# Layer 0: own scores and softmax of the next sequence ahead of the output products, output products in the projections' PSUM banks

## The reference, cut to what matters

```
xn   = layernorm(x)
q, k, v = xn Wq, xn Wk, xn Wv            # 8 heads of 64
own  = softmax(q k^T / 8) within segments of 32 rows, times v
mem  = elu1(q) . (sum over earlier segments of elu1(k)^T v) / (elu1(q) . z)     # elu1 = elu + 1
att  = sigmoid(beta) * mem + (1 - sigmoid(beta)) * own
h    = layernorm(gelu(xn Wfc)) * w + b;  s = h Wproj       # ternary Wfc, Wproj
x    = x + (s * sigmoid(s)) * (att Wo)
```

## Time and profile before

| | |
|---|---|
| median of 3 runs | 3017.87 us (3016.2 to 3020.25) |
| the profiled execution's own time | 3017.2 us |
| its span | 3015.1 us, of which layer 0's loop is about 79 to 575 us |
| TensorE, VectorE, ScalarE, GpSimd busy over the span | 83%, 77%, 57%, 11% |
| mean granted TensorE clock | 0.857 of full |

### The profile page before, as it was taken

How to read it: one execution, slowest core, us unless ns; L and a number is a source line. 1 busy time by engine, 2 the same in 40 slices (tenths; PEclk the granted TensorE clock), 3 DMA queues, 4 the chain that set the end, 5 groups by cost and what they waited for, 6 DMA issues and landing times. The chain is left out here.

```text
span 3015.1 us, 55454 instructions
## 1 busy us (share of the span) xinstructions
PE 2503.6 (83%) x18812; PEld 1895.3 (63%) x18812; DVE 2326.8 (77%) x6048; ACT 1709.8 (57%) x3452; POOL 329.3 (11%) x356
## 2 busy tenths in 40 slices
PE   1888888799999999967728888888888888988886
PEld 1555565577777777756725666666666666666665
DVE  2777777788788888767237888888888888888887
ACT  1676766565566565644325565565565655656554
POOL 0000000000000000023140111111111111111111
PEclk9999999899999999988857777777777778777778
DMA  7000000000000000030112334343333343432334
GB/s 215 1 0 0 0 0 0 0 1 1 1 0 0 1 0 1 1 82 14 56 43 76 94 85 106 92 107 98 80 78 87 96 106 92 106 91 78 86 86 112
DMA packets 86517, 163.71 MB, mean 54 GB/s; under 512 B 18856, under 2 KB 45616, under 8 KB 86320
## 3 DMA queue, kind: packets, MB, share of 16 engines
q0 software_dynamic: 20480, 62.93, 11.0%
q1 hardware_dynamic: 64640, 98.15, 10.0%
q10 hardware_dynamic: 1200, 0.27, 0.1%
HBM read 92.60 MB, written 9.99 MB: 34 GB/s over the span
## 5 line engine op out<-in xcount | busy, mean ns | idle before, releaser
L1132 ACT ACTIVATE b_neg<-b_neg,b_nmax 128x128 f32<-128x128 f32 (+1 forms) x512 | 190.9, 444 | 210.7 <-DVE b_nmax L1286 210.7
L2535 ACT ACTIVATE d_probs<-l_bank,w_b 128x256 f32<-128x256 f32 x512 | 210.2, 468 | 156.2 <-PE l_bank L2373 153.6
L2798 DVE TENSOR_TENSOR_SCAN d_state<-w,d_state 128x1024 f32<-128x1024 f32 x128 | 290.9, 2283 | 5.0 <-issue 3.7
L2373 PE MATMUL l_bank<-xnT,w_w 128*128 128x256 f32 x1024 | 245.1, 382 | 14.4 <-ACT d_probs L2535 14.4
L2384 PE MATMUL l_bank<-w_w,d_probs 128*128 128x128 f32 x2048 | 252.7, 276 | 0.0
L2384 PEld LDWEIGHTS l_bank<-w_w,d_probs 128*128 128x128 f32 x2048 | 244.9, 192 | 11.7 <-ACT d_probs L2535 5.3
L2303 PE MATMUL l_bank<-w 9*128 9x256 f32 x1040 | 207.5, 669 | 25.0 <-ACT w L2458 18.9
L2497 ACT ACTIVATE w<-d_delta,d_negA 128x255 f32<-128x255 f32 x520 | 220.2, 499 | 0.0
L94 POOL TENSOR_TENSOR ln_rstd<-ln_var_eps,minus_half 128x2 f32<-128x2 f32 x50 | 63.9, 1278 | 1405.0 <-DVE ln_var_eps L88 1405.0
L2373 PEld LDWEIGHTS l_bank<-xnT,w_w 128*128 128x128 f32 x1024 | 184.7, 190 | 41.1 <-ACT d_probs L2535 21.3
L2303 PEld LDWEIGHTS l_bank<-w 9*128 9x128 f32 x1040 | 122.3, 320 | 95.7 <-issue 29.9
(11 more groups left out here) (406 smaller groups left out, 5721.1 us busy)
## 6 DMA issues: line engine op xcount, KB each, us to landing
d_bct<-l_bc SPq DMA_DIRECT2D x132, 512.0 KB, 3.9
d_state<-d_state POOLq DMA_DIRECT2D x96, 512.0 KB, 6.6
d_state<-d_state POOLq DMA_DIRECT2D x32, 256.0 KB, 4.1
x_sorted<-x SPq DMA_DIRECT2D x1, 2560.0 KB, 16.5
w<-in_L_ffn_w_dram SPq DMA_DIRECT2D x1, 2048.0 KB, 9.6
w_w<-in_L_ffn_W_dram SPq DMA_DIRECT2D x1, 2048.0 KB
c2e_xg<-x_sorted SPq DMA_DIRECT2D x16, 128.0 KB
y_sorted<-c2e_yo SPq DMA_DIRECT2D x16, 128.0 KB, 1.8
```

Source lines behind the costliest of these rows:

```text
L1132: done = nc.scalar.activation(neg[:, slot, cols], neg[:, slot, cols], ACT.Exp, bias=nmax[:, slot, a:a + 1], scale=-1.0)
L2373: done = nc.tensor.matmul(bank[:, b, i * T:(i + 1) * T], w.w1[:, e, k * P:(k + 1) * P], x1T[:, :], start=True, stop=True)
L2535: done = v.activation(hid[:, e % 2, k, :], bank[:, b, i * T:(i + 1) * T], ACT.Gelu, bias=w.b1[:, e, k:k + 1])
L2798: done = v.tensor_tensor_scan(group, dA[i][:, g % (NG - 1), :, :].rearrange("p m t -> p (m t)"), group, 0.0, ALU.mult, ALU.add)
```

## The change

What it does, edit by edit:

1. `own_scores(n+1)` moves from the head of turn n+1 to the end of turn n, in front of `project_out(n)`. It now waits for `qk_taken` and for `hT_copied` of turn n (so that `ROW` is free). `turn_x` and `hidden` come first in the turn and `memory_scores(n, 1)` behind them.
2. `project_out` writes banks 0 and 1 in place of `ROW`, after `v_taken`. The projections of the next turn wait for `sz_taken`.
3. VectorE: `shift_scores(n+1)` and `divide_probs(n+1)` stand before u of turn n; `norm_stats` and `norm_apply` are done for n + 2, the former between the two `share_q`. Two `mask_memory` are placed one `elu_plus_1` or `times_z` earlier or later.
4. ScalarE: `exponentials(n+1)` before Tanh; `copy_xnT` before Gelu; three `copy_qk` before `apply_norm`; both `invert` before `copy_attT(1)`. The exp/tanh table is no longer loaded: gelu/tanh serves Tanh and the next Gelu.
5. `denominators(n+1, 1)` goes ahead of `heads_out(n, 3)`.
6. GpSimd does the norm power of n + 2 behind that of the hidden rows.
7. `c.x` has two more tiles (zeros, for the sequence behind the last). To make room, layer 3's `negA`, `recip`, statistics, router and combination buffers are laid over other buffers.

The diff, cut to its core:

```diff
@@ setup
-    c.x = sb_all("x", [P, TILES * (NSEQ + 1), D])
+    c.x = sb_all("x", [P, TILES * (NSEQ + 2), D])
@@ project_qk
-                    pe.wait_ge(v_taken, TILES * m + j - 1)
+                    pe.wait_ge(sz_taken, TILES * m + j - 1)
@@ own_scores
-            def own_scores():
+            def own_scores(m):
+                pe.wait_ge(qk_taken, NCH0 * m + NCH0)
+                if later(m):
+                    pe.wait_ge(hT_copied, TILES * m)
+                pe.sem_inc(pe_step, 1)
@@ project_out
                 pe.wait_ge(hT_copied, TILES * n + a + 1)
+                pe.wait_ge(v_taken, TILES * n + TILES + a + 1)
-                    nc.tensor.matmul(bank[:, ROW + a, 0:D], hT[:, a, j, :], c.wprojT[:, j, :],
+                    nc.tensor.matmul(bank[:, a, 0:D], hT[:, a, j, :], c.wprojT[:, j, :],
-                    done = nc.tensor.matmul(bank[:, ROW + a, D:2 * D], attT[:, j, a * P:(a + 1) * P], c.wo0[:, j, :],
+                    done = nc.tensor.matmul(bank[:, a, D:2 * D], attT[:, j, a * P:(a + 1) * P], c.wo0[:, j, :],
@@ TensorE's loop
+            own_scores(0)
                     n = 2 * m + par
-                    pe.wait_ge(qk_taken, NCH0 * n + NCH0)
-                    pe.wait_ge(sz_taken, TILES * n + TILES)
-                    pe.sem_inc(pe_step, 1)
-                    own_scores()
-                    memory_scores(n, par, 1)
+                    turn_x(n + 1)
                     for a in range(TILES):
                         hidden(n, par, a)
-                    turn_x(n + 1)
+                    memory_scores(n, par, 1)
...
                     heads_out(n, par, 2)
+                    denominators(n + 1, 1)
                     heads_out(n, par, 3)
-                    denominators(n + 1, 1)
                     memory_scores(n + 1, 1 - par, 0)
+                    own_scores(n + 1)
                     for a in range(TILES):
                         project_out(n, a)
@@ ScalarE's loop, as it is after
+                    copy_xnT(n + 1, 1 - par)
                     for a in range(TILES):
                         act.wait_ge(h_in_psum, TILES * n + a + 1)
                         v.activation(h[:, a, :], bank[:, ROW + a, :], ACT.Gelu).then_inc(gelu_done, 1)
                     load_exp_ln(nc)
+                    for j in range(3):
+                        copy_qk(n + 1, j)
                     act.wait_ge(hrstd_ready, n + 1)
                     for a in range(TILES):
                         apply_norm(a)
                     copy_qk(n + 1, 3)
+                    copy_attT(0)
                     for a in range(TILES):
                         copy_hT(a)
+                    for half in range(2):
+                        invert(n + 1, half)
                     copy_attT(1)
-                    load_exp_tanh(nc)
+                    exponentials(n + 1)
+                    load_gelu_tanh(nc)
@@ GpSimd's loop
             with pool.Fori(0, NSEQ) as n:
-                norm_power(nc, c, s, n + 1)
...
+                norm_power(nc, c, s, n + 2)
@@ VectorE's loop
-                    norm_stats(nc, c, s, n + 1)
...
                     elu_plus_1(n + 1, 1 - par, 0)
-                    mask_memory(n, 2)
                     elu_plus_1(n + 1, 1 - par, 1)
                     times_z(n + 1, 1 - par, 0)
+                    elu_plus_1(n + 1, 1 - par, 2)
+                    mask_memory(n, 2)
+                    elu_plus_1(n + 1, 1 - par, 3)
                     mask_memory(n, 3)
-                    elu_plus_1(n + 1, 1 - par, 2)
-                    elu_plus_1(n + 1, 1 - par, 3)
                     times_z(n + 1, 1 - par, 1)
                     for a in range(TILES):
                         take_v(n + 1, 1 - par, a)
                     share_q(n + 1, 1 - par, 0)
+                    norm_stats(nc, c, s, n + 2)
+                    share_q(n + 1, 1 - par, 1)
                     mask_memory(n + 1, 0)
-                    share_q(n + 1, 1 - par, 1)
+                    shift_scores(n + 1)
+                    norm_apply(nc, c, s, n + 2, False)
+                    divide_probs(n + 1)
                     for a in range(TILES):
                         dve.wait_ge(th_ready, TILES * n + a + 1)
@@ layer 3
-        negA = sb("negA", [P, CI, NS])
+        negA = w.A_log
-        recip = sb("recip", [P, TILES, H3])
+        recip = c.until[:, P - TILES * H3:].rearrange("p (a h) -> p a h", a=TILES)
...
```

More of the change, by code:

```diff
@@ L658, in invert, with exponentials @@
                 v.activation(rden[:, :, :].rearrange("p i t -> p (i t)"), lden[:, half, :], ACT.Exp, scale=-1.0).then_inc(rden_ready, 1)
+            def exponentials(m):
+                for odd in range(2):
+                    act.wait_ge(shifted_ready, 2 * m + odd + 1)
+                    rows = shifted[:, odd, :, :].rearrange("p h k -> p (h k)")
+                    v.activation(rows, rows, ACT.Exp, scale=DK0 ** -0.5).then_inc(exp_ready, 1)
             load_exp_ln(nc)
@@ L665, in _ @@
                 invert(0, half)
+            exponentials(0)
+            load_gelu_tanh(nc)
             with act.Fori(0, NSEQ // 2) as m:
@@ L761, in take_v, with mask_memory, shift_scores, dots @@
                 v.tensor_tensor(vmem[:, par, a, :], bank[:, a, :], c.gate[:, :], ALU.mult).then_inc(v_taken, 1)
+            def mask_memory(n, j):
+                dve.wait_ge(mem_scores, NCH0 * n + j + 1)
+                dve.wait_ge(out_done, NCH0 * n + j + NCH0 - 1)
+                v.tensor_tensor(memT[:, j % 2, :, :], bank[:, MEM:MEM + 2, 0:WIDE],
+                                c.mem_mask[:, :].unsqueeze(1).to_broadcast([P, 2, WIDE]), ALU.mult)\
+                    .then_inc(mem_masked, 1)
+            def shift_scores(m):
+                def dots(odd):
+                    return bank[:, ROW + odd, 0:AG * SEG].rearrange("p (h k) -> p h k", h=AG)
+                for odd in range(2):
+                    dve.wait_ge(scores_in_psum, 2 * m + odd + 1)
+                    v.tensor_reduce(top[:, odd, :], dots(odd), AX, ALU.max)
+                v.drain()
+                for odd in range(2):
+                    v.tensor_tensor(shifted[:, odd, :, :], dots(odd), bcast(top[:, odd, :], SEG), ALU.subtract)\
+                        .then_inc(shifted_ready, 1)
+            def divide_probs(m):
+                for odd in range(2):
+                    dve.wait_ge(exp_ready, 2 * m + odd + 1)
+                    v.tensor_reduce(total[:, :, odd], shifted[:, odd, :, :], AX, ALU.add)
+                v.drain()
+                v.reciprocal(recip[:, :, :], total[:, :, :])
+                v.drain()
+                for odd in range(2):
+                    v.tensor_tensor(shifted[:, odd, :, :], shifted[:, odd, :, :], bcast(recip[:, :, odd], SEG),
+                                    ALU.mult)
+                v.drain()
+            def turn_probs(odd):
+                for g in range(P // SEG):
+                    rows = slice(g * SEG, (g + 1) * SEG)
+                    done = v.transpose(probsT[rows, odd, :, rows], shifted[rows, odd, :, :])
+                return done
             v.memset(probsT[:, :, :, :].rearrange("p o g k -> p (o g k)"), 0.0)
@@ L778, in _ @@
                 take_v(0, 0, a)
[L779 to L784, removed]
             mask_memory(0, 0)
+            norm_stats(nc, c, s, 1)
+            shift_scores(0)
+            norm_apply(nc, c, s, 1, False)
+            divide_probs(0)
             with dve.Fori(0, NSEQ // 2) as m:
@@ L789, in _ @@
                     n = 2 * m + par
[L791 to L798, removed]
-                    norm_stats(nc, c, s, n + 1)
-                    for odd in range(2):
-                        dve.wait_ge(scores_in_psum, 2 * n + odd + 1)
-                        v.tensor_reduce(top[:, odd, :], dots(odd), AX, ALU.max)
-                    v.drain()
-                    for odd in range(2):
-                        v.tensor_tensor(shifted[:, odd, :, :], dots(odd), bcast(top[:, odd, :], SEG), ALU.subtract)\
-                            .then_inc(shifted_ready, 1)
-                    norm_apply(nc, c, s, n + 1, False)
-                    for odd in range(2):
-                        dve.wait_ge(exp_ready, 2 * n + odd + 1)
-                        v.tensor_reduce(total[:, :, odd], shifted[:, odd, :, :], AX, ALU.add)
-                    v.drain()
-                    v.reciprocal(recip[:, :, :], total[:, :, :])
-                    v.drain()
-                    for odd in range(2):
-                        v.tensor_tensor(shifted[:, odd, :, :], shifted[:, odd, :, :], bcast(recip[:, :, odd], SEG),
-                                        ALU.mult)
-                    v.drain()
                     turn_probs(0)
```

48 lines of the change are left out of this document (18 added, 30 removed).

## The result

The changed kernel takes 2949.8 us (median of 4 runs, 2948.4 to 2951.8) against 3018.8 us; the ratio is 0.9773, 95% interval 0.9756 to 0.9790, that is 68.9 us less. The forecast was 2953.

What follows compares the result with a forecast made beforehand. Hand-overs bound the kernel; afterwards VectorE would, at 25.8 + 0.7 = 26.5 us a turn. Sixteen turns from 86.0 end layer 0 at 510.0, not 574.8: 3017.2 - 64.8 = 2952.4, median 2953 us, range 2938 to 2983.

Steps and rivals of the forecast that it cites:

- The ring: Layer 0's hand-overs across engines set the 30.95 us turn; own scores, Tanh/u and copied x keep TensorE waiting.
- the bound: After the change VectorE's own 25.8 us a turn in layer 0 sets the pace; with waits 26.5 us.
- The two waits: VectorE still waits behind the hidden norm: 0.2 us at the last elu_plus_1, 0.5 us at mask_memory(n, 3).
- The pieces that the argument had going: TensorE's waits on Tanh/u, shifted scores and copied x go, 3.2 us a turn; the 1.1 us copy_attT wait too.
- B: A chain from hidden rows through statistics, last elu_plus_1 and invert to share_q 1 sets 29.0 us a turn, 2993 us; chance 0.15.
- C: TensorE's granted clock falls to 0.76 in layer 0, giving 32.2 us a turn and 3045 us; chance 0.04.
- D: u holds banks 0 and 1 and delays the next projections: 30.9 us a turn, 3018 to 3025 us; chance 0.04.
- The tables: One 1.28 us table load a turn goes from ScalarE, which has room; costed at nothing, bounds 0 and -0.2 us a turn.
- Edit 7: Changed buffer places leave layer 3's arithmetic and order the same: 0, bounds -3 and +3 us.
- The moved power: GpSimd's norm power, now beside share_q, takes 1.08 us and costs VectorE nothing; bounds 0 and +0.4 us a turn.
- The case that the prediction priced at 2964: If GpSimd's power takes the shared SBUF port before VectorE, a turn loses up to 0.7 us, 2964 in all.
- The first transpose: After the prologue's scores and softmax of sequence 0, layer 0's first transpose was put at 86.0 us.

Runs made afterwards that it cites:

- experiment 5: Changed kernel plus four bn_stats and three drains a turn on VectorE, before the mask of the next sequence's first memory scores; 2975.2 us, ratio 0.9857.
- 6: Kernel before the change plus four bn_stats and three drains a turn on VectorE, at the same mask; 3014.9 us, ratio 0.9986.
- 7: Changed kernel with the four TensorE products of memory scores 1 done twice each turn, 0.85 us more; 2952.8 us, ratio 0.9783.
- 9: Changed kernel with x + u done by GpSimd, behind its norm power, in place of VectorE; 2942.6 us, ratio 0.9752.
- experiment 10: Changed kernel with the norm statistics of n + 2 moved from between the two share_q to before the last elu_plus_1; 2946.8 us, ratio 0.9765.
- experiment 4: Changed kernel with the norm of x only one sequence ahead, at the head of VectorE's turn; 2998.9 us, ratio 0.9943.
- experiment 8: Changed kernel with the exp/tanh table for Tanh and a separate gelu/tanh load again, one more load a turn; 2950.5 us, ratio 0.9777.
- experiment 1: Kernel before the change with only the buffer places changed (two more tiles of x, layer 3's small buffers laid over others); 3017.2 us, ratio 1.0002.
- experiment 12: Changed kernel with the norm one sequence ahead and TensorE's memory scores 1 done four times in its wait; 2998.1 us, ratio 0.993.

## Why the prediction was right

**The ring and the bound.** VectorE was named as the bound at 25.8 us of its own a turn plus 0.7 of waits, 26.5 in all. The own scores of the trace are 26.37 us apart in the turn shown (215.15 to 241.52), and 26.45 is the mean behind the first turn. The two waits were put at 0.2 for the last `elu_plus_1` and 0.5 for `mask_memory(n, 3)`; they are 0.26 and 0.53. Experiments 5, 6, 7 and 9 show the bound: work added to VectorE shows in full after and not at all before, work taken off it shortens the turn by as much, and 0.85 us added to TensorE don't show. The pieces that the argument had going are gone from the waits of TensorE, as listed.

**Rivals.** B, a chain across engines in place of the ring, didn't come, but it is close: experiment 10 met its last part after a gain of 0.1 us a turn. With a late start of the projections (experiment 4) VectorE waited at the same hand-overs, the exponentials and the inversion, and the kernel took 2998.9 us, where B was put at 2993; there it was the late projections, and in part the clock, that made the chain late. C, the clock, went the other way: 1.00 in place of 0.94 in the late turns, with a lower clock in the first turn alone. D, banks 0 and 1 held by u, is seen in no wait of the projections.

**Edits at nothing.** The tables: 0.6 us (experiment 8). Edit 7: 0 (experiment 1). The moved power takes 1.06 us (put at 1.08), and the `share_q` beside it 0.69, so VectorE isn't held up. The Trainium skill, "SBUF — State Buffer", in the section "SBUF: two separate sides", has whichever of the two starts first hold the shared port and the other block. The trace agrees: `share_q` started 0.17 us before the power (241.20 and 241.37), GpSimd took 0.37 us longer than the 0.69 of the earlier trace rows, and VectorE lost nothing. The case that the prediction priced at 2964, GpSimd first, did not occur in the turn shown.

**What was off, by less than the range.** The gain in layer 0 is 62 us, not 64.8. The term mis-sized is the prologue and the first turn. The first transpose was put at 86.0 and came at 87.55, and the first turn took 28.5 us (transposes at 87.55 and 116.05) in place of 26.5. TensorE had sat idle for 4.4 us before it, where before the change it did memory scores and waited 1.24 us, and did its hidden rows at half speed:

```profile
85.64 0.69 PE L482 MATMUL l_bank<-ident,xn 128*128 128x128 f32 x2 [4.37 <-DVE xn L103]
86.12 3.62 PE L543 MATMUL l_bank<-wfcT,a_xnT 128*128 128x512 f32 x4
```

3.62 us against 1.88 later on. Its granted clock from 85.5 to 92.0 us was 0.53 on the mean, and VectorE waited 2.9 us for other engines in that turn in place of 0.8. Of the 1.55 us at the first transpose 0.7 are a later start (first own score at 79.95), which is within what the traces vary by. The other 15 turns, to the end of layer 0 at 512.85 us, took 26.45 us each. 1.55 + 2.0 - 15 x 0.05 = 2.8 us, and layer 0 ended 2.85 us later than forecast. The forecast's span, 3015.1 - 64.8 = 2950.3 us, was met within 0.2 us all the same, because layers 1 and 2, which no edit touches, were 3.7 us shorter in the profiled execution: that closeness is luck. The median is 3.2 us below the forecast of 2953; 2.0 of these are that the profiled execution was the slowest of the four.

**The parts.** The prediction gave no price to the single edits of the ring, and the runs show that none can be given: the norm's lead is worth 13 us alone and 49 us on top of the rest; the banks are worth 15 us on top of the rest. In a ring the last edit gets the credit. Three parts have no run of their own: the own scores and their softmax ahead of u, without the other edits; the new order of ScalarE's copies; and edit 5. What each gives by itself is not shown.

## What to carry to other kernels

Where every engine waits a little and none is full, follow one round of the hand-overs and subtract from its length each engine's waits: the largest remainder is the floor, and it was met here within 0.65 us a turn (25.8 and 26.45). Before filling an engine's last visible waits, ask which work in front of its other operands hides a chain that is just as long: the two waits of 0.8 us were worth 0.1. Work taken off the bounding engine (x + u to GpSimd) gave nearly all that it took, 0.56 of 0.6 us; work merely moved on it did not. And compare turn with turn: a first turn that is 2 us longer, or a loop that begins 1 us later, can hide or feign what an edit gives.

## What the runs showed of the hardware that was not expected

TensorE's clock fell in layer 0 behind short waits, and not behind each of them. With the late norm (experiment 4) TensorE waited 2.5 to 2.7 us in every turn behind the first. Over the 5 us behind that wait the mean granted clock was 0.50 to 0.68 of full in 14 of the 16 turns, that is wholly or partly at 1.2 in place of 2.4 GHz, and 1.00 in the other two. In the turn at 206 us two projections took 1.0 us longer for it. With work in that wait (experiment 12) the mean granted clock was 1.00 from 100 to 540 us. With work added to VectorE (experiment 5) the wait was 2.1 us on the mean in each turn, and only every fourth turn fell. So the length of the wait alone doesn't decide it. The Trainium skill, "TensorE: Matmul & The Clock Gate", Part 1, has activity release the throttle; the stretches of experiments 4 and 12 agree with it. In the kernel before, turns with the same instructions and the same waits in front of the hidden rows had 1.00 early and 0.94 late, for which no run here gives a reason.
